# One attention kernel: an earlier normalisation, another order of projection tiles, and the last shares by matrix products

## The reference

```python
x = x + xattn(layernorm(x), ctx, ctx)        # 16 heads of 32, rotary embedding, window 128
x = x + ffn(layernorm(x))                    # 512 -> 2048 -> 512, gelu
# xattn:
qp = rope(q @ wq.T); kp = rope(k @ wk.T); vp = v @ wv.T
scores = einsum('bhnqd,bhnkd->bhnqk', qb, kband) * sqrt(32)   # only |i-j| <= 128 kept
out = softmax(scores) @ vband
return out @ wo.T + wo_b
# ffn: weights rounded to 8 bits per channel, x and hidden rounded to 16 bits by their global maximum
```

## Time and profile before

| | us |
|---|---|
| median of 3 runs | 1254.26 |
| lowest and highest run | 1252.21, 1255.16 |
| the profiled execution | 1251.07 |
| its span, first to last instruction | 1249.3 |
| busy in the span: PE, DVE, ACT, POOL | 1138.1, 981.0, 639.6, 366.4 |

### The profile page before, as it was taken

How to read it: one execution, slowest core, us unless ns; L and a number is a source line. 1 busy time by engine, 2 the same in 40 slices (tenths; PEclk the granted TensorE clock), 3 DMA queues, 4 the chain that set the end, 5 groups by cost and what they waited for, 6 DMA issues and landing times.

```text
span 1249.3 us, 23318 instructions
## 1 busy us (share of the span) xinstructions
PE 1138.1 (91%) x7776; PEld 759.7 (61%) x7776; DVE 981.0 (79%) x2527; ACT 639.6 (51%) x1000; POOL 366.4 (29%) x540
## 2 busy tenths in 40 slices
PE   5889999999999899999999665999999979999997
PEld 5767777787777688677768443444444434444443
DVE  6769989989988988988899545666666678888885
ACT  5254355335435534543553243555655458777774
POOL 1136336344533634453363220000000030112220
PEclk9889999999999999999999787999999989999999
DMA  8453575566456447545644711455554400567762
GB/s 270 110 143 106 158 178 137 139 183 155 108 161 177 131 134 194 140 120 164 177 119 114 218 56 69 160 206 198 208 188 143 152 0 35 186 224 249 219 207 92
DMA packets 96055, 191.44 MB, mean 153 GB/s; under 512 B 13392, under 2 KB 24912, under 8 KB 95952
## 3 DMA queue, kind: packets, MB, share of 16 engines
q1 hardware_dynamic: 95952, 190.14, 51.5%
HBM read 89.43 MB, written 44.04 MB: 107 GB/s over the span
## 4 chain that ended last, share of the span: by engine, by line
PE 38%; DVE 31%; issue 24%; DMA 3%; SPq 2%; ACT 2%; POOL 0%; DVEq 0%; ACTq 0%; POOLq 0%
PE bank L792 17%; DVE bank L1063 6%; PE bank L514 4%; PE bank L515 4%; PE bank L516 4%; DVE bn L1024 3%; PE bank L597 2%; DVE roped L1089 2%; DVE neg_max L1104 2%; DVE rt L1086 2%; DVE row_max L1063 2%; DVE rt L1087 2%; DVE x_res L1056 1%; PE bank L526 1%; PE bank L581 1%
## 5 line engine op out<-in xcount | busy, mean ns | idle before, releaser
L1063 DVE CUSTOM_DVE_ANT_0 bank<-bank,mask 128x256 f32<-128x256 f32 x512 | 201.4, 454 | 54.6 <-PE bank L597 48.0
L792 PE MATMUL bank<-wout_int,g_hi 128*128 128x512 bf16 x512 | 195.8, 382 | 8.8 <-DVE g_lo L1336 8.7
L792 PE MATMUL bank<-wout_int,g_lo 128*128 128x512 bf16 x512 | 195.6, 382 | 0.0
L761 PE MATMUL bank<-qT_hi,win_int 128*128 128x512 bf16 x512 | 194.2, 379 | 1.4 <-DVE qT_lo L1254 1.4
L761 PE MATMUL bank<-qT_lo,win_int 128*128 128x512 bf16 x512 | 194.1, 379 | 0.0
L864 ACT ACTIVATE probs<-bank 128x512 f32<-128x512 f32 x256 | 142.4, 603 | 52.8 <-PE bank L631 48.3
L1381 POOL TENSOR_SCALAR_AFFINE_SELECT probs<-probs 128x256 f32<-128x256 f32 x256 | 109.1, 430 | 82.9 <-ACT probs L864 78.6
L1336 DVE TENSOR_TENSOR g_lo<-h_int,g_hi 128x512 f16<-128x512 f32 x128 | 104.3, 815 | 35.6 <-ACT g_hi L991 34.3
L597 PE MATMUL bank<-k_st,q_st 96*128 96x256 f32 x512 | 98.4, 306 | 25.7 <-DVE row_max L1063 19.3
L1374 POOL TENSOR_TENSOR x_res<-x_res,wo_b 128x512 f32<-128x512 f32 x32 | 42.0, 1332 | 243.9 <-DMA x_res<-in_x 231.1
L964 ACT ACTIVATE h_ring<-bank,b_in,g_scale 128x512 f32<-128x512 f32 x96 | 73.5, 778 | 75.2 <-PE bank L761 58.1
(11 more groups left out here) (146 smaller groups left out, 2666.2 us busy)
## 6 DMA issues: line engine op xcount, KB each, us to landing
hidden_scratch<-h_ring SPq DMA_DIRECT2D x96, 256.0 KB, 2.0
h_ring<-hidden_scratch SPq DMA_DIRECT2D x96, 256.0 KB, 3.0
k_st<-k_hi SPq DMA_DIRECT2D x128, 128.0 KB, 2.5
q_st<-q_hi SPq DMA_DIRECT2D x128, 128.0 KB, 2.4
xq<-x_scratch SPq DMA_DIRECT2D x16, 1024.0 KB, 6.2
x_ln<-in_x SPq DMA_DIRECT2D x16, 512.0 KB, 4.5
ctx_raw<-in_ctxT SPq DMA_DIRECT2D x16, 512.0 KB, 4.9
k_st<-k_lo SPq DMA_DIRECT2D x64, 128.0 KB, 2.7
```

The costliest lines, as they stand in the source:

```text
L761: mm = pe.matmul(bank[f % 4][:], win_int[:, c, f * P:(f + 1) * P], part[:, par, c], start=c == 0 and part is qT_hi, stop=c == KC - 1 and p ...
L792: mm = pe.matmul(bank[4 * par + u][:], part[:, f % 4, u * P:(u + 1) * P], wout_int[:, f], start=f == 0 and part is g_hi, stop=f == FC - 1 ...
L1063: dve.tensor_tensor_reduce(sc, sc, mask[:, (1 - qb) * P:(1 - qb) * P + S], 1.0, NEG, ALU.add, ALU.max, row_max[:, qb, n:n + 1]).then_inc(m ...
```

## The change

Five edits, all in stage A. (1) `normalise` of batch b - 1 stands in DVE's step behind pair 4 instead of pair 5. (2) On PE q's two tiles stand behind pairs 2 and 3 and v's first tile behind pair 4 (before: v's first, then q's two); on ACT the copy of v's first tile moves behind the leading parts of oT. (3) `stack_max` waits for the first of the two copies of the maxima only, and its three DMAs read one head's block four times instead of four heads' blocks. (4) Behind the last step the shares are no longer spread by DMA: PE multiplies den_r by a constant matrix `pick` of zeros and ones, four products of 256 columns in float32 into the two PSUM banks of the weighted values, and DVE multiplies oT by them. (5) `pick` (256 KB) is loaded once at the start.

```diff
     hot = np.tile((np.arange(HOT) % NC4 == NC4 - 1).astype(np.float32), (P, 1))
+    row, col = np.arange(P)[:, None], np.arange(P)[None, :]
+    pick = np.stack([row == DK * (col // DK) + i for i in range(NC4)], 1).astype(np.float32)
     sel = np.zeros((P, H), np.float32)
...
         sel[MROW + h, h] = sel[MROW + H + h, h] = 1.0
-    return {"c_rope": rope, "c_mask": mask, "c_sel": sel, "c_hot": hot, "c_ident": np.eye(P, dtype=np.float32)}
+    return {"c_rope": rope, "c_mask": mask, "c_sel": sel, "c_hot": hot, "c_pick": pick, "c_ident": np.eye(P, dtype=np.float32)}
...
         hot = sb("hot", [P, HOT], F32, pa)
+        pick = sb("pick", [P, NC4, P], F32, pa)
         x_ln = sb("x_ln", [P, 2, D], F32, pa)
...
-        c_in, rope_in, ident_in, b_out_in = sem("c_in"), sem("rope_in"), sem("ident_in"), sem("b_out_in")
+        c_in, rope_in, ident_in, pick_in, b_out_in = (sem(n) for n in ("c_in", "rope_in", "ident_in", "pick_in", "b_out_in"))
         w_in = {n: sem("in_" + n) for n in ("wk", "wq", "wv", "wo")}
...
         st_mm, exp_done, p_ready, pv_mm = sem("st_mm"), sem("exp_done"), sem("p_ready"), sem("pv_mm")
-        den_mm, den_done, den_out, share_in, oT_out, onorm = (
-            sem(n) for n in ("den_mm", "den_done", "den_out", "share_in", "oT_out", "onorm"))
+        den_mm, den_done, den_out, share_in, share_mm, oT_out, onorm = (
+            sem(n) for n in ("den_mm", "den_done", "den_out", "share_in", "share_mm", "oT_out", "onorm"))
         xres_b, res_done = sem("xres_b"), sem("res_done")
...
-                sp.wait_ge(mT_done, MAX_COPIES * (b + 1))
+                sp.wait_ge(mT_done, MAX_COPIES * b + 1)
                 for i in range(1, NC4):
                     sp.dma_start(q_st[MROW:P, KC * i:KC * (i + 1)].bitcast(F32),
-                                 q_st[MROW:P, 0:KC].bitcast(F32)).then_inc(max_stacked[i - 1], 16)
+                                 q_st[MROW:P, 0:1].bitcast(F32).to_broadcast([P - MROW, KC, S])).then_inc(max_stacked[i - 1], 16)
...
             load_ctx(2)
+            sp.dma_start(pick[:], t["c_pick"]).then_inc(pick_in, 16)
...
                 step(b, True, b + 1 < NB, b + 2 < NB, b + 3 < NB)
-            spread_shares(NB - 1)
             load_xres(NB - 1)
...
                     tiles[1] += [lambda: x_transposes(b + 1, 0), lambda: x_transposes(b + 1, 1), lambda: qk_tile(b + 1, "k", 1)]
-                    tiles[2] += [lambda: v_tile(b + 1, 0)]
-                    tiles[3] += [lambda: qk_tile(b + 1, "q", 0)]
-                    tiles[4] += [lambda: qk_tile(b + 1, "q", 1)]
+                    tiles[2] += [lambda: qk_tile(b + 1, "q", 0)]
+                    tiles[3] += [lambda: qk_tile(b + 1, "q", 1)]
+                    tiles[4] += [lambda: v_tile(b + 1, 0)]
                     tiles[5] += [lambda: v_tile(b + 1, 1, range(2))]
...
             steps(pe, step)
+            pe.wait_ge(pick_in, 16)
+            pe.wait_ge(den_done, NB)
+            for half in range(2):
+                pe.wait_ge(oT_out, 2 * NB - 1 + half)
+                for a in range(2):
+                    mm = pe.matmul(pv_bank[half][:, a * S:(a + 1) * S], pick[:, 2 * half + a], den_r, start=True, stop=True)
+                mm.then_inc(share_mm, 1)
             for _ in o_products(NB - 1, False):
...
                     xt_lead(b + 1, 1)
-                    v_copy(b + 1, 1 - par, 0)
                     split_hi("k", b + 1)
...
                 if has_proj:
+                    v_copy(b + 1, 1 - par, 0)
                     v_copy(b + 1, 1 - par, 1)
...
                     between[0] += [lambda: invert(b - 1)]
-                    between[5] += [lambda: normalise(b - 1, 0), lambda: normalise(b - 1, 1)]
+                    between[4] += [lambda: normalise(b - 1, 0), lambda: normalise(b - 1, 1)]
                 if has_proj:
...
             invert(NB - 1)
-            normalise(NB - 1, 0)
-            normalise(NB - 1, 1)
+            for half in range(2):
+                dve.wait_ge(share_mm, half + 1)
+                part = oT[:, 2 * half:2 * half + 2].rearrange("p i t -> p (i t)")
+                dve.tensor_tensor(part, part, pv_bank[half][:], ALU.mult).then_inc(onorm, 1)
             ot_rest(NB - 1, 0)
```

## The result

Before ran at 1253.24 us (median of 4 runs, 1250.35 to 1255.16), after at 1263.84 (median of 4, 1261.3 to 1264.42): the ratio is 1.0083, with a 95% interval of 1.0057 to 1.0108. The change made the kernel slower by 10.6 us; the forecast was 1262, 7.7 above the median it started from.

The account below looks back on a forecast made before the run. The attention steps were taken as a loop of DVE, then PE, then a handover, with no slack for a delay of the split. 11.3 + 1.9 - 4.3 - 0.6 = +8.3 on 1254.26 gave 1262 us, range 1251 to 1272.

Parts of the forecast that it names:

- Normalisation one pair sooner: Steps 1 to 14: DVE's normalisations meet POOL's k_lo, and PE's half tile then delays pair 7; +11.3 us in all.
- rival 2: Port free or nearly so, for instance DVE keeping its turn for both normalisations; 0.2 a step, total 0, 1254; chance 0.15.
- The 0.8: Predicted delay per step of the split of the maxima, 329.76 against 328.95, over 14 steps.
- q before v: PE's order of projection tiles: an exchange of equal lengths, cost 0, up to 0.1 a step either way.
- Maxima's rows: SP's three copies of the maxima may start 0.5 us sooner; gain between 0 and 1, taken as 0.6.
- The last step: Step b = 15: pair 5, formerly hidden before the end of the wait for the share, comes behind it; +1.9 us.
- The tail: Behind the last reciprocal: four fp32 products and two multiplications replace two DMAs and their landings; -4.3 us.
- The 2.5: Alternative gain for the last shares by products, with four products taking 3.4 by the page's two cycles a column at 1.2 GHz.
- +10.1: Alternative sum of the whole change if the last shares by products gain only 2.5.
- Rival 1: DVE loses the port once more, missing the first gap or held by a longer run; +18, 1272; chance 0.18.
- Rival 3: Faster: head 13's scores and the half tile do not hold; -7 in the steps, -3 elsewhere, 1244; chance 0.17.
- Rival 4: In the tail a reload of x_res takes the DMA path's place, so the -4.3 is lost; +12.6, 1267; chance 0.05.

Follow-up runs that it names:

- the first seven experiments: Early normalisation alone (1269.01), normalisation back (1247.79), port freed (1252.73), tile cut 3 + 1 (1254.26), both remedies (1250.54), cut with normalisation back (1249.22), tail alone (1248.1).
- the experiment in the last step: Changed kernel with the normalisations back behind pair 5, batch 14's shares in the last step made by PE products instead of DMA: 1244.89 us, ratio 0.9933.
- the last kernel: Changed kernel with normalisations back, batch 14's shares by products, and SP's two 1 MB loads issued behind the reload and shares: 1242.17 us, ratio 0.9912.

## Why the prediction was right, point by point

**Normalisation one pair sooner, +11.3 in fourteen steps: right in mechanism, and nearly in each time.** The fourteen steps took 13.0 more. Predicted for the two normalisations 1.87, measured 1.88; the split behind their start predicted 7.51 (329.76 - 322.25), measured 7.49; an idle stretch of 0.8 ahead of pair 7, measured 0.71; k_lo's four above 3.3, measured 3.72; reciprocals 44.5 apart, measured 44.74. The two experiments that freed the port and that shortened the tile show both links. The Trainium skill (SBUF — State Buffer, Who interferes with whom) says that the lock holds for an instruction, and not who is next. Here it was each in turn; rival 2's case, in which DVE keeps its turn for both, did not come.

The 0.8 was worked out from one step, and for such a step it is exact. That step's pair 4 starts 13.99 behind the reciprocal, near the median of the fourteen (14.05), and the predicted split is 23.00 behind it (329.76 - 306.76); the step of after whose pair 4 starts at 14.01 has its split at 23.00. As a mean of fourteen steps it was off on both sides. The mechanism cost 9.9 at the splits (8.1 and 1.8, above) where 11.3 was booked, since not every step has its pair 4 that late, and an undisturbed one costs 0.58. The late share, booked at nothing, cost 4.4: I had called its landing safe (321.4 against 322.25) from a median of 3.7, and in four steps it wasn't, for 1.6 us of waiting and the rest behind it. That 11.3 came so near to 13.0 is in part luck. No run brings the share's DMA forward, so its part is read from the rows alone.

Two slips of the working did no harm. At 1100 us the two DVE instructions last 1.06 and 1.01 longer than the same lines do alone (medians of 0.69 and 0.48), which is less than a whole POOL instruction (2.55 / 2 = 1.28 in the earlier trace rows). And a product at twice the transposes' row adds 1.76 for four, which leaves the tail a gain of 2.3 to 2.5, and not 2.7.

**q before v, 0: right.** The tail alone gives the gain of all four parts. **Maxima's rows, -0.6: nothing seen.** The copies landed in 2.4 instead of 2.3 us, and PE's waits on them went from 2.0 to 0.5 (1.4 in the kernel with the normalisation back); any gain is under what the runs can tell.

**The last step, +1.9: right, beside 1.7 that it did not foresee.** Pair 5 behind the wait cost 1.99 (26.83 - 20.06 = 6.77 from the normalisations to the split, before 23.56 - 18.78 = 4.78), as worked out. Of the rest, the 1.3 ahead of the normalisations is the share landing later behind the two large loads: 7.3 us from one issue to the next in the profile before and 8.8 in after. In the seven profiles of the first seven experiments it is 7.4 to 9.1, with no order by where the normalisation stands (7.4 with the early one alone, 8.5 with it back), so I take it for scatter of this transfer. The remaining 0.35, behind the split, stays unexplained.

**The tail, -4.3: right, by a price and a clock that were both wrong.** Measured -4.19, and 5 us in two experiments. I took 0.44 for a product, from fp32 transposes at the half clock. PE ran at the full clock there (window 761.50 to 765.00: 1.00), and a product took 0.43 at that clock, so twice my row's price at equal clock. The Trainium skill (FP8 and Floating Point Precision, TensorE Precision Notes) counts four passes for true fp32; the trace agrees, 256 columns at four cycles and 2.4 GHz being 0.43. The 2.5 that I worked out from the page assumed the half clock too, which is why my 4.3 came out nearer for the tail. The whole sum that went with it, +10.1, lies nearer to the measured 10.6 than my 8.3, but only because other terms were too small.

**Rivals.** Rival 1 (a POOL instruction more) didn't come in any step of the trace that had landed shares; in two of the four steps with a share wait the split did slip a further 0.9 to 1.0, but not by a POOL instruction: the pair of normalisations lasted 2.10 and 2.01, and the greater part (0.73 and 0.87) is PE's half tile at the lower clock. Rival 3 (faster) is excluded by every kernel with the early normalisation: even with both links cut it stands above the kernel with the normalisation back (1250.54 against 1247.79), and the 0.71 ahead of pair 7 shows that head 13's scores and the half tile do hold. Rival 4 didn't come in the tail, but its mechanism, the reload of x_res behind other transfers, is what stopped the experiment in the last step.

## What to carry to other kernels

Idle time ahead of an instruction is not free room: it takes up the lateness of whatever varies upstream, and work put there passes that lateness on, beside its own length. Work that is moved forward also asks for its inputs sooner: a transfer that lands in time by its median may be late in some steps, and here four such steps cost 4.4 us, against 1.8 for the lateness that the idle time no longer took up. Before moving work on an engine that shares a port, lay the neighbour's instructions over its new place; and before hoping for the room it leaves, look for the next wait of the chain, here half a tile of PE. A cheap gain of this study, 4.2 us by moving three lines, was in the order of one DMA queue: what is waited for goes ahead of what is large.

## What the runs showed of the hardware

A true fp32 product of 128 x 128 by 256 columns is recorded as two, and takes 0.43 us at the full clock; in the last step of the kernel with products there, where the granted clock was 0.62 from 705 to 709.5 us, four of them took 3.30, so 0.83 each. At the lower level alone, as in the last kernel, the eight records stand 0.43 apart (706.98 to 709.97), so 0.85 a product. A score product of 256 columns takes 0.12 (four in 0.48). That price mattered little in the tail, where PE had nothing else to do, and did in the last step, where the scores' chain runs through PE.

Where two instructions of DVE met four of POOL, both sides paid: DVE 0.59 and POOL 0.89 for the meeting. Taking POOL out of the way cost nothing (its four ran in 2.82 again, behind the normalisations, and nobody waited for them).

A late input to DVE can be followed by a lower clock of PE: in two of the four steps in which PE stood still for 1.15 to 1.39 us ahead of head 12's scores, the granted clock was 0.50 for 3.4 us behind it. The kernel with the early normalisation alone shows it once (1.25 of idle time, 0.50 from 198.1 to 201.5). The records don't say why it fell in some of these steps and not in others.

A transfer of 128 KB issued behind two of 1 MB landed in 7.3 to 9.1 us in nine kernels (8.8 in after), and in 3.8 with these behind it.
